# Output matmuls ahead of the scores of their pair, expert blocks written out, new orders in the prologue

## The chip, the cores and the metric

The kernel runs on one NeuronCore of one Trainium2 chip. The metric is the device time of one execution in microseconds (us); lower is better. Times of the engines come from one execution recorded by the hardware profiler.

## The reference

One layer: cross attention of 2048 latents on 1601 context rows and on the latents themselves, then a mixture of experts. All numbers are float32.

```python
# x: (1, 2048, 256), ctx: (1, 1601, 192), mask: (1, 1601)
xn = layernorm(ctx, ln_x_g, ln_x_b)
ln = layernorm(_layernorm(x), ln_l_g, ln_l_b)
q = ln @ Wq.T
kv = concatenate([xn @ Wkv.T, ln @ Wlkv.T], axis=1)      # 1601 + 2048 keys
qn = rmsnorm(q, qn_g) * 64 ** -0.5                        # 4 heads of 64
kn = rmsnorm(k, kn_g)
attn = softmax(where(full_mask, qn @ kn.T, -max))
x = x + (attn @ v) @ Wo.T + bo
h = _layernorm(x)
probs = softmax(h @ router_w.T)                           # 8 experts
weights, indices = top_k(probs, 2); weights = weights / (sum + 1e-6)
gate, up = split(h @ w13[e]);  y = (silu(gate) * up) @ w2[e]
x = x + sum over the two experts of weight * y
```

## The kernel before

Keys are padded to 29 tiles of 128 (13 of context, 16 of latents). The kernel has three stages, each written as one instruction stream per engine, with semaphores between the streams. Each engine runs its own stream strictly in order: an instruction that waits holds all behind it. Nothing is planned at run time; all orders are those of the code.

**Prologue** (0 to about 150 us). For each of the 29 tiles, in a pipeline: VectorE normalises rows (`apply`), TensorE transposes them into bX, ScalarE copies them to xT with scale and bias, TensorE projects them (bA: keys and queries, bV: values), ScalarE squares the keys (bSq), VectorE sums (`ss`), ScalarE takes the root (`nrm`), VectorE divides (knat, qn), TensorE transposes the keys (bK), ScalarE copies them to S2 (`s2`), and GpSimd copies their high part into S1 (`keys_hi`) while VectorE forms the low part (`klo`). Each engine has its own function `pro` (TensorE from L1327, ScalarE from L671, VectorE from L945), called with a step s; a part of a later stage works on tile s-2, s-3 or s-4. TensorE's projections wait for `xT` of the tile and for `knat` of the tile two before. Then GpSimd clears half of Q2 (L519, L521, semaphore `q20`), and TensorE computes the first unit's score maxima.

**Attention** (about 150 to 790 us). 16 units: 4 blocks of 512 queries times 4 heads. A unit has 15 steps p, each with a pair of key tiles (the last with one). In a step TensorE computes `scores(p)` into one of two double banks bS (two matmuls per tile, L1474 and L1475), ScalarE takes the exponential of the pair into PT (one of four buffers, L824), and GpSimd or VectorE adds PT to the running sums of the denominators (acc_p, acc_d). `outputs(p)` multiplies PT with V into bPV (L1485; a float32 matmul is seen as two records). TensorE does outputs in twos: at each odd p above 1 those of p-3 and p-2; the last three at the unit's end. Outputs of p wait for the exponential of p; scores of p wait for that of p-2.

Besides, unit v = u+1 needs the maximum of its scores beforehand. Therefore 32 `pieces` (L1401) of 464 keys for 128 queries are computed during unit u, into two banks bM in turn, and VectorE reduces each to a maximum (L1041, mpart). A piece waits until the reduction of the piece two before it is done:

```python
pe.wait_ge(sem("m_red"), NM * v + k + 1 - len(banks))
```

`PIECES` gives two counts for each step, `pieces(p, 0)` and `pieces(p, 1)`:

```python
PIECES = ((1, 0), (2, 0)) + ((1, 0), (2, 2)) * 5 + ((2, 0), (2, 0), (0, 0))
```

After the last piece VectorE forms the maximum (L1047), TensorE transposes it (`c_T`, L1407) and ScalarE copies it (`c_row`), on which the next unit's first scores wait. Other small work of the previous head or block is put at fixed steps: the transposed outputs and their division at 5 (`o_T` L1416, `o_out` L1053 and L1058), heads at 7, the output projection of one tile at 8, its second layer norm at 8 to 10, its transposes at 11, the router's logits at 12. On VectorE these come ahead of the reductions of their step. The last unit has no pieces; there VectorE also does all sums of the denominators and a part of the routing.

**Experts** (about 793 to 1045 us). The 4096 pairs of token and expert, sorted by expert, are 39 blocks of 128 rows. GpSimd gathers a block's rows (xg), TensorE transposes them (bXe, L1633), computes gate and up (bG, bU), transposes the product (bH, L1612) and computes bY (L1595 to L1597 are the three products of `three`); GpSimd adds the rows to the output by a scatter. TensorE reads the expert's number from `eid` into a register and addresses the weights W with it. `eid` packs three following numbers in base 8; blocks 5 to 38 are a hardware loop (`Fori`) of 17 passes with two blocks and one such read.

Of the kernel before, what the change touches and what calls it, by code (L numbers as in the profile page):

```python
# [4 lines left out]
F32 = mybir.dt.float32  # L5
# [4 lines left out]
ALU = mybir.AluOpType  # L10
ACT = mybir.ActivationFunctionType
AX = mybir.AxisListType.X

P = 128
# [115 lines left out]
def build(nc, x, ctx_in, mask, ln_x_g, ln_x_b, ln_l_g, ln_l_b, qn_g, kn_g, w_lat, w_ctx, wo_t, bo,  # L130
# [13 lines left out]
    with stack:  # L144
# [314 lines left out]
        def _(pool):  # L459
# [42 lines left out]
            for t in range(NK + 2):  # L502
                if t < NC + 2:
                    k_mask(t)
                    pool.wait_ge(sem("kmask"), t + 1)
                if t + 4 < NK:
                    rest_zero(t + 4, t + 5)
                    pool.wait_ge(sem("s20"), t + 2)
                if t == 3:
                    pool.wait_ge(sem("c_bo"), 16)  # L510
                    pool.wait_ge(sem("x_in"), 16)
                if 3 <= t < 3 + NT:
                    x_bias(t - 3)
                    pool.wait_ge(sem("xb"), t - 2)
                if t >= 2:
                    keys_hi(t - 2)
                    pool.wait_ge(sem("s1"), t - 1)
            pool.wait_ge(sem("v_mm"), NK)
            pool.memset(Q2[D:P, :, :].bitcast(F32), 0.0).then_inc(sem("q20"), 1)  # L519
            pool.wait_ge(sem("q20"), 1)  # L520
            pool.memset(Q2[D:D + 2, :, :].bitcast(F32), 1.0).then_inc(sem("q20"), 1)  # L521
            pool.wait_ge(sem("q20"), 2)
# [135 lines left out]
        def _(act):  # L658
            act.dma_start(wc[0:P, 0, :], w_ctx[0:P, :]).then_inc(sem("wc_in"), 16)
            act.dma_start(wc[0:CIN - P, 1, :], w_ctx[P:CIN, :]).then_inc(sem("wc_in2"), 16)  # L660
            for n, g in enumerate((ln_x_g, ln_x_b)):
                for k in range(2):
                    r = min(P, CIN - k * P)
                    act.dma_start(cols[0:r, 2 * n + k:2 * n + k + 1],
                                  g[k * P:k * P + r].rearrange("(p a) -> p a", a=1)).then_inc(sem("cols"), 16)

# [4 lines left out]
            def pro(s, a, b, c, q=0):  # L671
                if a:
                    act.wait_ge(sem("xT_mm"), s.v + 1)
                    if not (s.i is None and s.off < 2):
                        act.wait_ge(sem("v_mm"), s.v - 1)
                    for k in range(2):
                        r = P if (k == 0 or a == 'l') else CIN - P
                        g0 = 0 if a == 'c' else 4
                        act.activation(xT[0:r, s.par, k, :], bX[s.par][0:r, 0, k * P:(k + 1) * P], ACT.Identity,  # L679
                                       scale=cols[0:r, g0 + k:g0 + k + 1], bias=cols[0:r, g0 + 2 + k:g0 + 3 + k])\  # L680
                            .then_inc(sem("xT"), 1)
# [14 lines left out]
                if b:  # L696
                    act.wait_ge(sem("v_mm"), t.v + 1)
                    if b == 'l':
                        act.wait_ge(sem("xb"), t.back(NC).v + 1)
                    act.copy(V[:, bass.ds(t.v, 1), :].rearrange("p a d -> p (a d)"), bV[t.par][:, 0, 0:DIM])\  # L700
                        .then_inc(sem("v_cp"), 1)
                if q:
# [8 lines left out]
                if b:  # L711
                    lo = 0 if b == 'l' else H
                    act.wait_ge(sem("ss"), t.v + 1)
                    act.activation(nrm[:, lo:2 * H], ss[:, lo:2 * H], ACT.Sqrt, scale=1.0 / D)\
                        .then_inc(sem("nrm"), 1)
# [189 lines left out]
        def _(dve):  # L905
# [378 lines left out]
            link(dve.scalar_tensor_tensor(zt[:, 0:w], ef[:, 2:NBLK], float(E * E), zt[:, 0:w], ALU.mult, ALU.add))  # L1284
            dve.tensor_copy(eid[:], zt[:]).then_inc(sem("routed"), 1)
# [38 lines left out]
        def _(pe):  # L1324
# [134 lines left out]
            def unit(w):  # L1459
# [46 lines left out]
                for p in range(NP):  # L1506
                    scores(p)
# [16 lines left out]
                    if p % 2 and p > 1:  # L1524
                        outputs(p - 3)
                        outputs(p - 2)
# [73 lines left out]
            def experts(b):  # L1600
                v = pe.value_load(eid[0:1, bass.ds(b, 1)], min_val=0, max_val=E ** 3 - 1)
                return v % E, v // E % E, v // (E * E)
# [43 lines left out]
            e0, e1, _ = experts(0)  # L1646
            ffn(Step(None, 1), 1, 1, 0, e0, None)
            ffn(Step(None, 2), 1, 1, 1, e1, e0)
            e1, e2, e3 = experts(1)
            ffn(Step(None, 3), 1, 1, 1, e2, e1)  # L1650
            ffn(Step(None, 4), 1, 1, 1, e3, e2)
            with pe.Fori(0, (NBLK - 5) // 2) as i:
                eh, eg, en = experts(2 * i + 3)
                ffn(Step(i, 5), 1, 1, 1, eg, eh)
                ffn(Step(i, 6), 1, 1, 1, en, eg)
            eh, eg, _ = experts(NBLK - 2)
            ffn(Step(None, NBLK), 0, 1, 1, eg, eh)
            ffn(Step(None, NBLK + 1), 0, 0, 1, None, eg)

# [12 lines left out]
RING_FROM = 5  # L1672
POOL_SUMS = ((0, 1),) + tuple((-1, p) for p in (2, 3, 6, 7, 8, 10, 11, 12))
# [35 lines left out]
```

## Time and profile before

| | before |
|---|---|
| time, median of 3 runs (us) | 1047.28 (1045.42 to 1048.57) |
| profiled execution: its own time / its span (us) | 1047.05 / 1045.2 |
| TensorE matmuls busy | 965.9 us, 92% |
| TensorE weight loads busy | 626.4 us, 60% |
| VectorE busy | 695.8 us, 67% |
| ScalarE busy | 488.5 us, 47% |
| GpSimd busy | 593.6 us, 57% |
| mean granted TensorE clock, share of full speed | 0.978 |
| chain that ended last | PE 71%, DVE 10%, issue 6%, DMA 5%, ACT 4% |

PE is TensorE's matmuls, PEld its weight loads, DVE VectorE, ACT ScalarE, POOL GpSimd. The span is from the first to the last recorded instruction; the execution's own time has some 2 us around it. Matmuls overlap in the records, so a matmul's own duration is longer than the distance to the next. The chain is the work that ended last, followed back from the end; in it each matmul has the time that it adds.

### The profile page before, as it was taken

To read this page: it belongs to the slowest core of one execution; us is meant where nothing else is said; L and a number is where in the kernel's file an instruction comes from. 1 tells how busy PE (TensorE), PEld (TensorE's weight loads), DVE (VectorE), ACT (ScalarE), POOL (GpSimd) and SP (SyncE) were. 2 spreads that over 40 slices of the span, in tenths; PEclk is the share of its full clock that TensorE was granted. 3 is DMA by queue.
4 is the path that set the end of the run, shared out by engine and by line. 5 is a ranking of instruction groups with operands and counts; after the bars stand their busy time and mean duration, and the time that the engine had idled before them with its cause. 6 is when DMAs were issued, how large, how long until landed. Compare 5 with 4: busy or idle time off the path is not lost.

```text
span 1045.2 us, 15560 instructions
## 1 busy us (share of the span) xinstructions
PE 965.9 (92%) x4571; PEld 626.4 (60%) x4572; DVE 695.8 (67%) x1353; ACT 488.5 (47%) x782; POOL 593.6 (57%) x497
## 2 busy tenths in 40 slices
PE   5798779999999999999999999999997799999994
PEld 4555445556556555556556656565555687778883
DVE  5977677776776776776776776767786544444442
ACT  3565534554555465555555645655552232222231
POOL 2553227677677667666776676676800355555552
PEclk9999979999999999999999999999997999999998
DMA  6110021112122122222221221221248467663332
GB/s 188 40 37 6 18 87 66 57 61 68 54 66 76 61 76 72 65 66 64 74 71 61 66 81 56 72 75 62 94 179 302 129 161 165 153 136 54 53 52 25
DMA packets 72479, 87.51 MB, mean 84 GB/s; under 512 B 11399, under 2 KB 65608, under 8 KB 71400
## 3 DMA queue, kind: packets, MB, share of 16 engines
q1 hardware_dynamic: 56424, 70.73, 20.7%
q0 software_dynamic: 7488, 10.39, 6.2%
q10 hardware_dynamic: 8512, 5.71, 1.8%
q8 instruction: 28, 0.46, 0.2%
q14 instruction: 27, 0.22, 0.1%
HBM read 50.03 MB, written 36.77 MB: 83 GB/s over the span
## 4 chain that ended last, share of the span: by engine, by line
PE 71%; DVE 10%; issue 6%; DMA 5%; ACT 4%; POOL 2%; ACTq 1%; POOLq 0%; DVEq 0%
PE bPV L1485 20%; PE bM L1401 10%; PE bS L1474 9%; PE bS L1475 8%; DVE mpart L1041 2%; PE bA L1344 2%; DMA xg<-xln_d,ring_g 2%; ACT PT L824 2%; PE bT L1416 2%; PE bG L1595 1%; PE bY L1595 1%; PE bY L1597 1%; PE bY L1596 1%; PE bH L1612 1%; PE bV L1361 1%
## 5 line engine op out<-in xcount | busy, mean ns | idle before, releaser
L1041 DVE TENSOR_REDUCE mpart<-bM 128x1 f32<-128x464 f32 x490 | 294.5, 635 | 127.1 <-PE bM L1401 125.7
L535 POOL TENSOR_TENSOR acc_p<-acc_p,PT 128x1024 f32<-128x1024 f32 x120 | 302.9, 2524 | 103.8 <-ACT PT L824 100.4
L824 ACT ACTIVATE PT<-bS 128x1024 f32<-128x1024 f32 (+1 forms) x240 | 237.5, 997 | 199.8 <-PE bS L1475 170.6
L1485 PE MATMUL bPV<-PT,V 128*64 128x512 f32 x928 | 230.6, 604 | 0.0
L1474 PE MATMUL bS<-QQ,S 128*128 128x512 f32 x464 | 189.5, 408 | 3.6 <-ACT QQ L745 1.1
L1475 PE MATMUL bS<-QQ,S 128*128 128x512 f32 x464 | 183.7, 396 | 0.0
L1401 PE MATMUL bM<-S,QQ 128*128 128x464 f32 x490 | 172.2, 410 | 7.2 <-DVE mpart L1041 7.1
L1401 PEld LDWEIGHTS bM<-S,QQ 128*128 128x128 f32 x490 | 84.3, 191 | 90.3 <-DVE mpart L1041 69.8
L1485 PEld LDWEIGHTS bPV<-PT,V 128*64 128x64 f32 x928 | 58.7, 136 | 104.4 <-issue 92.3
L1474 PEld LDWEIGHTS bS<-QQ,S 128*128 128x128 f32 x464 | 87.7, 189 | 55.3 <-issue 26.7
L1475 PEld LDWEIGHTS bS<-QQ,S 128*128 128x128 f32 x464 | 87.8, 189 | 14.1
L539 POOL TENSOR_TENSOR wraw<-wraw,whi 128x256 fp32r<-128x256 f32 x96 | 85.2, 888 | 12.3 <-ACT whi L779 12.3
L1073 DVE TENSOR_TENSOR acc_d<-acc_d,PT 128x1024 f32<-128x1024 f32 (+1 forms) x58 | 88.3, 1523 | 1.3 <-ACT PT L824 0.6
L535 POOL TENSOR_TENSOR acc_p<-PT 128x1024 f32<-128x1024 f32 x15 | 38.4, 2559 | 86.9 <-ACT PT L824 86.9
L779 ACT CAST whi<-wraw 128x256 fp32r<-128x256 f32 x96 | 38.5, 402 | 84.5 <-DMA wraw<-w 83.9
L642 POOL DMA_INDIRECT out<-ysb,ring_s x34 | 54.4, 1601 | 34.5 <-POOL ring_s L635 23.0
L1298 DVE TENSOR_TENSOR hs<-hs,bU 128x512 f32<-128x512 f32 x39 | 26.8, 688 | 62.8 <-PE bU L1597 56.6
L886 ACT CAST hTe<-bH 128x512 fp32r<-128x512 f32 x39 | 22.9, 586 | 69.0 <-PE bH L1612 47.3
L618 POOL DMA_INDIRECT xg<-xln_d,ring_g x34 | 34.4, 1012 | 27.1 <-POOL ring_g L614 27.1
L1595 PE MATMUL bY<-W,hTe 128*128 x156 | 47.2, 303 | 1.5 <-DVE hTe L1292 1.5
L679 ACT ACTIVATE xT<-bX,cols 128x128 f32<-128x128 f32 (+1 forms) x58 | 23.2, 452 | 45.5 <-PE bX L1332 41.7
L1596 PE MATMUL bY<-W,hTe 128*128 x156 | 44.0, 282 | 0.0
(246 smaller groups left out, 1467.8 us busy)
## 6 DMA issues: line engine op xcount, KB each, us to landing
wraw<-w SPq DMA_DIRECT2D x96, 128.0 KB, 2.4
wsp_d<-whi SPq DMA_DIRECT2D x96, 128.0 KB, 2.4
wsp_d<-wraw SPq DMA_DIRECT2D x96, 128.0 KB, 1.7
W<-wsp_d SPq DMA_DIRECT2D x8, 1536.0 KB, 9.2
W<-wsp_d SPq DMA_DIRECT2D x32, 384.0 KB
V<-x SPq DMA_DIRECT2D x1, 2048.0 KB, 11.3
xb_d<-xbs SPq DMA_DIRECT2D x16, 128.0 KB, 1.7
x<-xb_d ACTq DMA_DIRECT2D x12, 128.0 KB, 2.0
```

The lines of the kernel that those rows point to most:

```text
L535: pool.tensor_tensor(acc_p[:], one, PT[:, q % NPT, :, :], ALU.add).then_inc(sem("z_p"), 1)
L539: pool.tensor_tensor(wraw[:, n % 2, :].bitcast(F32R), wraw[:, n % 2, :], whi[:, n % 2, :].bitcast(F32), ALU.subtract).then_inc(sem("wsplit ...
L642: pool.indirect_dma_start(out, bass.IndirectOffsetOnAxis(ap=rows, axis=0), ysb[:, s.par, :], None, compute_op=ALU.add)\
L824: act.activation(PT[:, p % NPT, 0:n, :], bS[(w.h + p) % 2][:, 0:n, :], ACT.Exp).then_inc(sem("exp"), 1)
L1041: dve.tensor_reduce(mpart[:, i, g:g + 1], banks[k % len(banks)][:, 0:PIECE], AX, ALU.max)\
L1073: dve.tensor_tensor(acc_d[:, 0:m, :], one, PT[:, q % NPT, 0:m, :], ALU.add).then_inc(sem("z_d"), 1)
L1401: pe.matmul(banks[k % len(banks)][:, 0:PIECE], Q2[:, h % 2, i * P:(i + 1) * P], S2[:, h, g * PIECE:(g + 1) * PIECE], start=True, stop=True ...
L1474: pe.matmul(bS[sl][:, b, :], S1[:, h, c * P:(c + 1) * P], Q1[:, h % 2, :], start=True, stop=False)
L1475: last = pe.matmul(bS[sl][:, b, :], S2[:, h, c * P:(c + 1) * P], Q2[:, h % 2, :], start=False, stop=True)
L1485: last = pe.matmul(bPV[b * D:(b + 1) * D, 0, :], V[:, c, h * D:(h + 1) * D], PT[:, p % NPT, b, :], start=c < 2, stop=c >= NK - 2, skip_gro ...
L1595: pe.matmul(out_ap, st_hi, w[:, s, 0, lo:lo + n], start=first, stop=False)
L1596: pe.matmul(out_ap, st_lo, w[:, s, 0, lo:lo + n], start=False, stop=False)
```

## The change

Five parts:

1. Attention, TensorE: in every unit `outputs(p-3)` and `outputs(p-2)` stand ahead of `scores(p)` instead of between `pieces(p, 0)` and `pieces(p, 1)`. `PIECES` and the banks stay.
2. Experts, TensorE: the loop is replaced by all blocks written out; a read of `eid` brings five expert numbers (8 reads). VectorE packs two more numbers into `eid`.
3. Prologue, ScalarE's `pro`: squares, key copy, norm, value copy, then the tile's copy xT, then queries. Before: xT first and the norm last.
4. Prologue, ScalarE's DMA issues: the four column loads ahead of the two of wc.
5. Prologue, GpSimd: the clears of Q2 at loop step 28, ahead of `keys_hi(26)`, instead of behind the loop.

```diff
@@ gpsimd
+                if t == NK - 1:
+                    pool.wait_ge(sem("v_mm"), NK)
+                    pool.memset(Q2[D:P, :, :].bitcast(F32), 0.0).then_inc(sem("q20"), 1)
+                    pool.wait_ge(sem("q20"), 1)
+                    pool.memset(Q2[D:D + 2, :, :].bitcast(F32), 1.0).then_inc(sem("q20"), 1)
+                    pool.wait_ge(sem("q20"), 2)
                 if t >= 2:
                     keys_hi(t - 2)
                     pool.wait_ge(sem("s1"), t - 1)
-            pool.wait_ge(sem("v_mm"), NK)
-            pool.memset(Q2[D:P, :, :].bitcast(F32), 0.0).then_inc(sem("q20"), 1)
...
@@ scalar
-            act.dma_start(wc[0:P, 0, :], w_ctx[0:P, :]).then_inc(sem("wc_in"), 16)
-            act.dma_start(wc[0:CIN - P, 1, :], w_ctx[P:CIN, :]).then_inc(sem("wc_in2"), 16)
             for n, g in enumerate((ln_x_g, ln_x_b)):
...
+            act.dma_start(wc[0:P, 0, :], w_ctx[0:P, :]).then_inc(sem("wc_in"), 16)
+            act.dma_start(wc[0:CIN - P, 1, :], w_ctx[P:CIN, :]).then_inc(sem("wc_in2"), 16)
...
             def pro(s, a, b, c, q=0):
-                if a:
-                    act.wait_ge(sem("xT_mm"), s.v + 1)
...
                 if b:
+                    lo = 0 if b == 'l' else H
+                    act.wait_ge(sem("ss"), t.v + 1)
+                    act.activation(nrm[:, lo:2 * H], ss[:, lo:2 * H], ACT.Sqrt, scale=1.0 / D)\
+                        .then_inc(sem("nrm"), 1)
+                if b:
                     act.wait_ge(sem("v_mm"), t.v + 1)
...
+                if a:
+                    act.wait_ge(sem("xT_mm"), s.v + 1)
...
@@ vector
+            for n in (3, 4):
+                w = NBLK - n
+                link(dve.scalar_tensor_tensor(zt[:, 0:w], ef[:, n:NBLK], float(E ** n), zt[:, 0:w], ALU.mult, ALU.add))
             dve.tensor_copy(eid[:], zt[:]).then_inc(sem("routed"), 1)
@@ tensor
                 for p in range(NP):
+                    if p % 2 and p > 1:
+                        outputs(p - 3)
+                        outputs(p - 2)
                     scores(p)
...
                     pieces(p, 0)
-                    if p % 2 and p > 1:
-                        outputs(p - 3)
-                        outputs(p - 2)
                     pieces(p, 1)
...
-            def experts(b):
-                v = pe.value_load(eid[0:1, bass.ds(b, 1)], min_val=0, max_val=E ** 3 - 1)
-                return v % E, v // E % E, v // (E * E)
+            order = []
+            def experts():
+                v = pe.value_load(eid[0:1, len(order):len(order) + 1], min_val=0, max_val=E ** AHEAD - 1)
+                for n in range(AHEAD):
+                    order.append((v // E ** n if n else v) % E)
...
-            with pe.Fori(0, (NBLK - 5) // 2) as i:
-                eh, eg, en = experts(2 * i + 3)
-                ffn(Step(i, 5), 1, 1, 1, eg, eh)
-                ffn(Step(i, 6), 1, 1, 1, en, eg)
...
+            for b in range(1, NBLK + 2):
+                if len(order) < min(b + 1, NBLK):
+                    experts()
+                ffn(Step(None, b), b < NBLK, b <= NBLK, b > 1, order[b - 1], order[b - 2])
+AHEAD = 5
```

## Rows read from the trace of the kernel before

**Rows 1.** Waits of TensorE, 155 to 790 us: total us, times, longest.

```profile
PE bM L1401 <- DVE mpart L1041: 6.9, 12, 1.9
```

**Rows 2.** Busy us by window: length, PE, PEld, DVE, ACT, POOL, granted clock, DMA.

```profile
0.00:50.00 50.00, 33.40 (x153) 24.23 (x155) 36.99 (x133) 23.29 (x68) 20.73 (x49) 1.00 0.38 117
...
100.00:110.00 10.00, 9.20 (x38) 5.33 (x37) 6.56 (x17) 6.51 (x18) 1.72 (x3) 1.00 0.00 0
...
140.00:150.00 10.00, 6.17 (x15) 3.31 (x15) 6.88 (x16) 3.08 (x5) 1.45 (x2) 0.50 0.30 95
```

**Rows 3.** Chain of waits, steps 5 to 7 of a unit: start us, us added.

```profile
357.06 0.53 PE bM L1401 x2
357.58 1.87 PE bPV L1485 x8
359.45 0.62 PE bM L1401 x2
...
362.13 0.42 PE bM L1401 x2
```

**Rows 4.** Timeline, step 13 and step 5: start us, us, instruction, idle before and releaser.

```profile
338.80 0.78 PE L1401 MATMUL bM<-S,QQ 128*128 128x464 f32 x2
...
339.21 1.19 DVE L1041 TENSOR_REDUCE mpart<-bM 128x1 f32<-128x464 f32 x2
340.44 0.19 DVE L1047 TENSOR_REDUCE cells<-mpart 128x4 f32<-128x32 f32 x1
340.54 3.69 DVE L1073 TENSOR_TENSOR acc_d<-acc_d,PT 128x1024 f32<-128x1024 f32 x2
...
357.31 0.42 DVE L1058 TENSOR_TENSOR on<-bT,cells 128x256 f32<-128x256 f32 x1
```

**Rows 5.** Timeline around a piece of step 9 that waits.

```profile
367.95 1.82 DVE L1041 TENSOR_REDUCE mpart<-bM 128x1 f32<-128x464 f32 x3
...
368.61 0.19 PEld L1401 LDWEIGHTS bM<-S,QQ 128*128 128x128 f32 x1 [0.86 <-DVE mpart L1041]
368.61 0.47 PE L1401 MATMUL bM<-S,QQ 128*128 128x464 f32 x1 [0.45 <-DVE mpart L1041]
...
369.02 1.94 PE L1485 MATMUL bPV<-PT,V 128*64 128x512 f32 x8
```

**Rows 6.** Timeline of TensorE, step 2 to step 3.

```profile
348.71 0.38 PE L1401 MATMUL bM<-S,QQ 128*128 128x464 f32 x1
349.22 0.50 PE L1474 MATMUL bS<-QQ,S 128*128 128x512 f32 x1
```

**Rows 7.** Timeline of VectorE, last unit, first sum.

```profile
763.75 1.23 DVE L1073 TENSOR_TENSOR acc_d<-PT 128x1024 f32<-128x1024 f32 x1 [3.38 <-PE bT L1417]
```

**Rows 8.** Timeline of TensorE, prologue: projections of latent tiles.

```profile
56.32 1.95 PE L1344 MATMUL bA<-wl,xT 128*128 128x512 f32 x4
...
104.74 1.95 PE L1344 MATMUL bA<-wl,xT 128*128 128x512 f32 x4 [0.71 <-ACT xT L679]
108.27 1.95 PE L1344 MATMUL bA<-wl,xT 128*128 128x512 f32 x4
```

**Rows 9.** Timeline, end of the prologue: first piece and first reduction.

```profile
127.94 1.91 PE L1401 MATMUL bS<-S,QQ 128*128 128x464 f32 x4 [3.20 <-POOL QQ L521]
...
128.73 2.28 DVE L1041 TENSOR_REDUCE mpart<-bS 128x1 f32<-128x464 f32 x4 [2.16 <-PE bS L1401]
```

**Rows 10.** Waits of TensorE, experts, 830 to 1030 us: total us, times, longest.

```profile
PE bH L1612 <- issue: 4.8, 10, 0.6
```

**Rows 11.** Timeline of TensorE, experts: transposes of single blocks.

```profile
941.29 0.60 PE L1612 MATMUL bH<-ident,hs 128*128 128x128 f32 x4
...
1002.67 0.60 PE L1612 MATMUL bH<-ident,hs 128*128 128x128 f32 x4
1007.54 0.60 PE L1612 MATMUL bH<-ident,hs 128*128 128x128 f32 x4
...
1023.30 0.63 PE L1612 MATMUL bH<-ident,hs 128*128 128x128 f32 x4
```

More of the change, by code:

```diff
@@ L517, in _ @@
                     pool.wait_ge(sem("s1"), t - 1)
-            pool.wait_ge(sem("v_mm"), NK)
-            pool.memset(Q2[D:P, :, :].bitcast(F32), 0.0).then_inc(sem("q20"), 1)
-            pool.wait_ge(sem("q20"), 1)
-            pool.memset(Q2[D:D + 2, :, :].bitcast(F32), 1.0).then_inc(sem("q20"), 1)
-            pool.wait_ge(sem("q20"), 2)
             NZ = len(POOL_SUMS)
@@ L671, in pro @@
             def pro(s, a, b, c, q=0):
-                if a:
-                    act.wait_ge(sem("xT_mm"), s.v + 1)
[L674 to L681, printed above, removed]
                 if b:
@@ L701, in pro @@
                         .then_inc(sem("v_cp"), 1)
+                if a:
+                    act.wait_ge(sem("xT_mm"), s.v + 1)
+                    if not (s.i is None and s.off < 2):
+                        act.wait_ge(sem("v_mm"), s.v - 1)
+                    for k in range(2):
+                        r = P if (k == 0 or a == 'l') else CIN - P
+                        g0 = 0 if a == 'c' else 4
+                        act.activation(xT[0:r, s.par, k, :], bX[s.par][0:r, 0, k * P:(k + 1) * P], ACT.Identity,
+                                       scale=cols[0:r, g0 + k:g0 + k + 1], bias=cols[0:r, g0 + 2 + k:g0 + 3 + k])\
+                            .then_inc(sem("xT"), 1)
                 if q:
@@ L710, in pro @@
                                    ACT.Identity, scale=gT[:, 0:1]).then_inc(sem("qT"), 1)
[L711 to L715, printed above, removed]
             lo, hi = CTX_LOADS[0]
@@ L1645, in _ @@
             pe.wait_ge(sem("routed"), 1)
[L1646 to L1651, printed above, removed]
-            with pe.Fori(0, (NBLK - 5) // 2) as i:
-                eh, eg, en = experts(2 * i + 3)
-                ffn(Step(i, 5), 1, 1, 1, eg, eh)
-                ffn(Step(i, 6), 1, 1, 1, en, eg)
-            eh, eg, _ = experts(NBLK - 2)
-            ffn(Step(None, NBLK), 0, 1, 1, eg, eh)
-            ffn(Step(None, NBLK + 1), 0, 0, 1, None, eg)
+            for b in range(1, NBLK + 2):
+                if len(order) < min(b + 1, NBLK):
+                    experts()
+                ffn(Step(None, b), b < NBLK, b <= NBLK, b > 1, order[b - 1], order[b - 2])
 CTX_LOADS = ((0, 4), (4, NC - 1))
```

## Prediction

> **What bounds the kernel now.** I read the page first: TensorE is busy 966 us of 1045 (the table above), and what it waits for in the attention stage (155 to 790 us) is almost nothing; the table of waits puts 6.9 us down to the reductions of the piece maxima, its largest item [rows 1]. So there an instruction that TensorE runs costs its length, a new wait costs in full, and a mere change of order is worth only the waits it removes. The stage is 16 units of 38 to 41 us, seen as the starts of their last output matmuls. Then I read the chain of waits through one pair of steps. Output matmuls of two steps take 1.87, two pieces after them 0.62, and two pieces before them 0.42: a piece is 0.21, and 0.20 is paid once on leaving the outputs. The pair of steps repeats after 357.58 to (362.13 + 0.42) = 4.97, without a gap [rows 3].
>
> **Attention: where four pieces now meet.** A step's pieces are two counts, (2, 2) at steps 3, 5, 7, 9 and 11; the outputs stood between the two. Now outputs come before the scores, and the four pieces follow each other. There are two bM banks, and piece k waits until the reduction of k-2 is done. Before, 1.87 us of outputs covered two reductions. Worked out from the first piece's start at 0, with nothing between them:
> - the reduction of a starts 0.41 later (338.80 to 339.21), and one takes 0.61 (1.82 for three) [rows 4, 5]: a is free at 1.02, b at 1.63;
> - c starts at 1.06 and d at 1.68: 0.05 after a reduction ends (the first of the three from 367.95 ends at 368.56, the waiting piece starts at 368.61);
> - a piece that waited takes 0.41 until the next matmul (368.61 to 369.02), not 0.21, as its weight load starts with it [rows 5]. The next scores start at 2.09.
>
> Four pieces unhindered take 0.84, so a group loses 1.25. The 0.20 on leaving the outputs is then paid by the scores: no change. Bounds: 1.0 if both loads were hidden, 1.35 if a reduction's start slips a little. At step 5 VectorE first runs the division of the finished head: it ends at 357.73, 0.67 after the piece that the chain has at 357.06 [rows 3, 4], so a's reduction starts about 0.3 later and that group loses 1.55 (in 14 of the 15 units that have pieces). A pieces' unit loses 4 x 1.25 + 1.55 = 6.55.
>
> The weight load has a rule. The row shows the load of the waiting piece at 368.61, not earlier [rows 5]. The Trainium skill, TensorE: Matmul & The Clock Gate, "Architectural detail: the array is 16x 32x32, not 1x 128x128", says that TensorE's queue can pull weight loads ahead of matmuls in flight. By it both loads would hide and the total would be 75 x 2 x 0.2 = 30 us lower, an estimate; the row speaks against it, as the wait holds the load too.
>
> **Attention: the end of a unit.** Step 13 had pieces, outputs 10 and 11 (1.87), scores 14, then the transposes of the maxima. Its two pieces now end the piece work directly ahead of scores 14 (0.46, two matmuls). VectorE ends the second reduction at 0.41 + 1.22 = 1.63 and its maximum of 0.19 follows [rows 4] at about 1.85; TensorE is there at 0.42 + 0.46 = 0.88. That is 1.0 of wait. From there outputs 12 to 14 (2.7) lead to the next unit, while VectorE still has two sums (3.69 [rows 4]) and two merges (some 1.9 more, by the same rate). Its first reduction comes some 0.6 late and holds the second piece of step 1: another 0.5. So 1.55 per unit, from 0.6 to 2.2.
>
> **Attention: what the order gives back.** Scores 3 wait for exp 1 at the start of a unit: the piece at 348.71 would be done at 348.92, scores start at 349.22 with a slower first one [rows 6]; the outputs of step 0 now fill this: 0.4 in 15 units. The piece at step 9 that waits at 368.61 (VectorE is behind with the statistics of step 8) has outputs ahead of it now: the wait of 0.45 and the load of 0.2 go, 0.7 in 11 units. Step 13's pieces cost 0.2 more than free ones, 15 times. Unit 0 has one wait of 1.9 of the same kind. Together 6 + 7.7 + 3 + 1.9 = 18.6.
>
> Sum for units 0 to 14: 15 x 6.55 - 0.3 + 15 x 1.55 - 18.6 = +102.6. In the last unit, which has no pieces, VectorE's first sum waits for the transposed output of step 5 and starts at 763.75 after 3.38 idle [rows 7]. Two outputs (1.87) now stand before that, and the exponentials wait for the sums. But step 11's wait for the normalised tile then covers the same 1.87. I take +0.7, from -1.5 to +2.5. Attention: +103.
>
> **Prologue.** For latent tiles TensorE starts a tile every (104.74 - 56.32) / 12 = 4.03 us; where it waits for nothing the distance is 108.27 - 104.74 = 3.53 [rows 8]. The loop is: ScalarE waits for the transpose of tile s before it squares tile s-2, the norm comes last in its step, and TensorE waits for the normalised key. In the new order squares, key copy and norm come first, and the tile copy behind them needs only what is there; ScalarE and VectorE, busy 6.5 and 6.6 us in 10 [rows 2], so 2.6 per tile of 4.03, stay below 3.53 with their gaps closed. Behind the tile copy wait TensorE's projections, one step later, with 1 us to spare. 15 tiles x 0.45 = 6.5, from 2 to 7.5. Context tiles: the timeline has VectorE, which also does the statistics of x there, without a gap from 24 to 47 us, so nothing there; an estimate of 1.5 in the last three and 1 at the start, by the gaps VectorE has in them. The DMA order: the columns' loads go ahead of wc and land perhaps 1 us sooner, wc (384 KB) is queued later behind x and may land 1 to 1.5 after the columns. Net 0, between -1.5 and +1.5. The Q2 clears: the first pieces wait for them at 127.94 after 3.20 idle, the first reduction is at 128.73 [rows 9]. They now run as soon as the last V matmul is done (about 119.5), while GpSimd waits for keys; the three key copies behind them can slip by the clears' 1.9 and catch up, as each waits for ScalarE. What then sets the first reduction is VectorE's own key and query work, free 2.16 before it [rows 9]: gain 2.1, up to 3.1, nothing if these copies are late. Prologue: -11, from -4 to -14.
>
> **Experts.** Loop passes show as idle before the first transposes of odd blocks: 4.8 us in 10 gaps, "issue", up to 0.6 [rows 10], and the load exposed beside them. Undisturbed blocks are 1007.54 - 1002.67 = 4.87 apart; 16 blocks from 941.29 to 1023.30 take 5.13 each, 4.1 in all over the floor [rows 11]. The first 18 blocks lose about as much again to it and also wait for gathers, which GpSimd and the weight DMAs set; there a removed gap mostly turns into a longer gather wait. Eight loads of the expert numbers stay, at a gap of about 0.4 each. So 3 from the second half, 1 from the first: -4, from +3 (straight code served worse than the loop) to -8. Two more VectorE instructions of 0.2 before "routed" lie beside the first gather. The end is a chain of scatters that follows TensorE: it moves with it.
>
> The gap itself: by the row 0.2 to 0.6 at a pass. The Trainium skill, Advanced Engine Details and Errata, "Control Flow Timing", gives about 51 ns for a branch and 108 ns for a compare and branch; 17 passes would be an estimated 2.7 us, and the written out code would bring 1 us instead of 4. The rows say that more than the branch is lost.
>
> **Sum.** +103 - 11 - 4 = +88 on the profiled execution: span 1045.2, its own time 1047.05, which is 0.2 below the median of the three runs. 1047 + 88 = 1135.
>
> **Rivals.**
> - *The pieces don't hold the queue* (faster). If scores could start past a waiting piece, four pieces in a row would be free, and the returned waits (18.6), prologue and experts would remain: 1047 - 19 - 11 - 4 = 1013. It decides from the point at which VectorE is at most 0.5 behind TensorE at a group's end. For it: VectorE is only 67% busy. Against: at 368.61 the outputs, which need nothing of that piece, waited behind it [rows 5]. 4%.
> - *One wait in a group, not two*: if reduction a started with its bank's own end, c would hardly wait; 0.6 per group instead of 1.25: 75 x 0.65 = 49 less, 1086. Row 339.21 is against it. 7%.
> - *The clock.* If the new gaps lowered the granted clock, TensorE would run at 1.2 GHz of 2.4 in part. It was 0.50 in 140 to 150, a window in which TensorE was busy 6.2 us and waited long for the last reductions, and 1.00 over the first 50 us with 33 us busy [rows 2]. My gaps are up to 1.2. A tenth of the stage at half speed adds about 60: 1195. 4%.
> - *The unit's end recovers nothing and reductions slip*: everything at its upper bound in attention, 75 x 0.1 + 15 x 0.65 = +17, and half the prologue's gain: 1158. 10%.
>
> My forecast has 75%. For the range: the likeliest with its bounds runs from 1112 to 1152; I widen it a little to 1106 and 1156, which leaves out the rivals at 1013, 1086 and 1195 and part of the last. A difference below 0.3% (3 us) can't be told from none. Faster 0.05, same 0.01, slower 0.94.
>
> **What would show it.** The waits table of after: "PE bM from DVE mpart" at 70 to 100 us instead of 7, in some 150 places, with two of about 0.6 in a group; the pair of steps at 6.2 instead of 4.97; a unit at 45 to 48; latent tiles 3.5 to 3.6 apart; the first reduction of unit 0 about 10 us earlier; no idle time before transposes of experts except at one block in five. The forecast is wrong if the four pieces stand in the timeline without gaps, if the pair of steps stays near 5, or if the granted clock in attention is below 1.

## The result, and the profile after

| | before | after |
|---|---|---|
| median of the runs, us | 1046.57 | 1135.74 (1135.29 to 1136.63) |
| ratio after / before | | 1.085, interval 1.083 to 1.087 |
| span of the profiled execution, us | 1045.2 | 1133.5 |
| mean granted TensorE clock | 0.978 | 0.961 |

The changed kernel is 8.5% slower; 1135 was predicted. The stages of the two traces, each from one mark to the next (the "end" of a unit is the start of its ten last output matmuls):

| stretch | before | after | difference | predicted |
|---|---|---|---|---|
| start to the first reduction of a piece | 128.7 | 113.4 | -15.3 | -11 |
| to the end of unit 0, then of unit 14 | 57.5 + 564.3 | 62.0 + 660.7 | +4.5 + 96.4 | +102.6 |
| to the first output of the tail (last unit) | 42.5 | 46.1 | +3.6 | +0.7 |
| tail and router to the first gather | 26.1 | 26.1 | 0 | 0 |
| experts | 226.0 | 225.2 | -0.8 | -4 |

The sum is right to 1 us, but three of its terms (prologue, last unit, experts) were not, as the last two columns show, and inside attention's term errors met that the section on the prediction takes apart. First the waits of TensorE in attention after (total us, times, longest), against [rows 1]:

```profile
PE bM L1405 <- DVE mpart L1042: 41.3, 73, 0.8
PE bT L1411 <- DVE cells L1048: 13.6, 15, 0.9
PE bS L1478 <- ACT PT L825: 3.6, 3, 2.5
```

The wait of a piece for the reduction of the piece two before it went from 6.9 to 41.3 us, and a wait of the transposes of the maxima (bT), 0.9 in each of 15 units, is new. The rest of the loss is not in this table, because it is in weight loads. The timeline of a group of four shows it (start us, us, instruction, idle before and releaser); it is to be read beside [rows 3, 5] of the kernel before:

```profile
367.40 0.58 PE L1405 MATMUL bM<-S,QQ 128*128 128x464 f32 x2
...
367.81 2.40 DVE L1042 TENSOR_REDUCE mpart<-bM 128x1 f32<-128x464 f32 x4 [2.23 <-PE bM L1405]
368.50 0.19 PEld L1405 LDWEIGHTS bM<-S,QQ 128*128 128x128 f32 x1 [0.91 <-DVE mpart L1042]
368.50 1.02 PE L1405 MATMUL bM<-S,QQ 128*128 128x464 f32 x2 [0.52 <-DVE mpart L1042]
...
369.05 0.19 PEld L1405 LDWEIGHTS bM<-S,QQ 128*128 128x128 f32 x1 [0.36 <-DVE mpart L1042]
...
369.36 0.39 PE L1478 MATMUL bS<-QQ,S 128*128 128x512 f32 x1
```

Two pieces run, the third stands until the first reduction is over (0.52), the fourth issues its load late too (PEld row 369.05). From the first piece to the scores it is 369.36 - 367.40 = 1.96 us; four free pieces take 0.84. The load of a piece that waits starts with it, at 368.50 as in [rows 5]: the pull-ahead of the Trainium skill (TensorE: Matmul & The Clock Gate, "Architectural detail: the array is 16x 32x32, not 1x 128x128") does not reach past a wait of this kind here either.

At step 5 VectorE's division of the finished head comes first, and in this unit the clock then falls:

```profile
375.20 0.67 PE L1405 MATMUL bM<-S,QQ 128*128 128x464 f32 x2
375.59 0.42 DVE L1059 TENSOR_TENSOR on<-bT,cells 128x256 f32<-128x256 f32 x1
...
376.61 1.30 PE L1405 MATMUL bM<-S,QQ 128*128 128x464 f32 x2 [0.75 <-DVE mpart L1042]
377.71 0.63 PE L1478 MATMUL bS<-QQ,S 128*128 128x512 f32 x1
378.14 0.63 PE L1479 MATMUL bS<-QQ,S 128*128 128x512 f32 x1
```

The group takes 2.51, 1.67 more than a free one. From 377.71 the scores are 0.43 apart, before they were 0.23 (a matmul's record 0.63 against 0.39). The windows (length, PE, PEld, DVE, ACT, POOL, granted clock, DMA) say why, the granted clock being 0.86 in the first and 1.00 in the next. Taken by single us it is 0.50 from 377 to 380:

```profile
370.00:382.00 12.00, 11.21 (x49) 6.12 (x48) 5.60 (x10) 3.38 (x4) 4.62 (x4) 0.86 0.21 67
382.00:394.00 12.00, 10.82 (x44) 6.14 (x44) 7.02 (x15) 6.09 (x8) 8.17 (x5) 1.00 0.18 60
```

The wait of 0.75 alone does not decide it. In unit 1 of the same trace the group of step 5 starts at 192.56 and has the same wait, but the granted clock stays 1.00 (190 to 197 us), the group takes 2.28 and the scores behind it are 0.23 apart:

```profile
192.56 0.67 PE L1405 MATMUL bM<-S,QQ 128*128 128x464 f32 x2
193.98 1.02 PE L1405 MATMUL bM<-S,QQ 128*128 128x464 f32 x2 [0.75 <-DVE mpart L1042]
194.84 0.40 PE L1478 MATMUL bS<-QQ,S 128*128 128x512 f32 x1
```

Units 2 and 4 are like unit 1; in the other 11 of the 14 units with this wait the clock falls. What else it takes stays open.

The unit's end, beside [rows 4] (DVE L1048 is the maximum over the pieces, L1074 the sums, L1411 the transposes that wait for the maximum):

```profile
404.80 1.94 DVE L1074 TENSOR_TENSOR acc_d<-acc_d,PT 128x1024 f32<-128x1024 f32 x2
405.03 0.60 PE L1411 MATMUL bT<-ident,cells 128*1 128x128 f32 x4 [0.91 <-DVE cells L1048]
```

The two sums take 1.94 here and took 3.69 before, because there the first began while GpSimd was running two of its own (337.16 to 342.00), as this row of the kernel before shows; *e5_three* below says what that does:

```profile
337.16 4.84 POOL L535 TENSOR_TENSOR acc_p<-acc_p,PT 128x1024 f32<-128x1024 f32 x2
```

Prologue and last unit, against [rows 8, 9] and [rows 7]: the first and the last latent tile, the first reduction, the first sum of the last unit.

```profile
52.16 1.88 PE L1348 MATMUL bA<-wl,xT 128*128 128x512 f32 x4
...
103.15 1.88 PE L1348 MATMUL bA<-wl,xT 128*128 128x512 f32 x4
...
113.41 1.17 DVE L1042 TENSOR_REDUCE mpart<-bS 128x1 f32<-128x464 f32 x2
...
851.27 1.23 DVE L1074 TENSOR_TENSOR acc_d<-PT 128x1024 f32<-128x1024 f32 x1 [6.35 <-PE bT L1421]
```

### The profile page after: what moved, and what is told of

It reads as the page before. It is cut to its first block, busy times and chain, and to the rows that moved or that the text cites. A ratio compares the mean times of both kernels' runs of the same rounds, so it can differ in the third digit from the quotient of the medians.

```text
span 1133.5 us, 15379 instructions
## 1 busy us (share of the span) xinstructions
PE 1007.7 (89%) x4571; PEld 628.6 (55%) x4571; DVE 673.1 (59%) x1355; ACT 484.7 (43%) x782; POOL 578.4 (51%) x497
## 4 chain that ended last, share of the span: by engine, by line
PE 65%; DVE 16%; DMA 8%; issue 6%; POOL 2%; ACT 1%; POOLq 1%; ACTq 0%; DVEq 0%
PE bPV L1489 20%; PE bS L1478 12%; DVE mpart L1042 10%; PE bS L1479 9%; PE bM L1405 8%; DMA xg<-xln_d,ring_g 4%; PE bA L1348 3%; DMA out<-ysb,ring_s 2%; PE bV L1365 2%; PE bT L1420 1%; POOL ring_g L615 1%; DMA out<-ysb,sidx 1%; PE bT L1421 1%; PE bT L1432 1%; PE bT L1411 1%
## 5 line engine op out<-in xcount | busy, mean ns | idle before, releaser
L1405 PE MATMUL bM<-S,QQ 128*128 128x464 f32 x490 | 192.6, 435 | 47.3 <-DVE mpart L1042 42.3
L1489 PE MATMUL bPV<-PT,V 128*64 128x512 f32 x928 | 234.6, 613 | 0.0
L1478 PE MATMUL bS<-QQ,S 128*128 128x512 f32 x464 | 201.1, 434 | 4.7 <-ACT PT L825 3.6
L1479 PE MATMUL bS<-QQ,S 128*128 128x512 f32 x464 | 189.0, 407 | 0.0
L1405 PEld LDWEIGHTS bM<-S,QQ 128*128 128x128 f32 x490 | 92.6, 196 | 112.3 <-DVE mpart L1042 100.3
L1478 PEld LDWEIGHTS bS<-QQ,S 128*128 128x128 f32 x464 | 90.8, 196 | 108.8 <-issue 80.1
L1479 PEld LDWEIGHTS bS<-QQ,S 128*128 128x128 f32 x464 | 90.8, 196 | 14.0
L540 POOL TENSOR_TENSOR wraw<-wraw,whi 128x256 fp32r<-128x256 f32 x96 | 70.8, 738 | 14.4 <-ACT whi L780 14.4
L1074 DVE TENSOR_TENSOR acc_d<-acc_d,PT 128x1024 f32<-128x1024 f32 (+1 forms) x58 | 62.2, 1072 | 1.4 <-ACT PT L825 0.6
L1599 PE MATMUL bY<-W,hTe 128*128 x156 | 47.5, 305 | 1.5 <-DVE hTe L1296 1.5
L619 POOL DMA_INDIRECT xg<-xln_d,ring_g x34 | 34.4, 1013 | 27.1 <-POOL ring_g L615 25.5
L1601 PE MATMUL bY<-W,hTe 128*128 x156 | 44.0, 282 | 0.0
L1600 PE MATMUL bY<-W,hTe 128*128 x156 | 44.0, 282 | 0.0
```

Of the source, the lines that this page charges most:

```text
L540: pool.tensor_tensor(wraw[:, n % 2, :].bitcast(F32R), wraw[:, n % 2, :], whi[:, n % 2, :].bitcast(F32), ALU.subtract).then_inc(sem("wsplit ...
L1074: dve.tensor_tensor(acc_d[:, 0:m, :], one, PT[:, q % NPT, 0:m, :], ALU.add).then_inc(sem("z_d"), 1)
L1405: pe.matmul(banks[k % len(banks)][:, 0:PIECE], Q2[:, h % 2, i * P:(i + 1) * P], S2[:, h, g * PIECE:(g + 1) * PIECE], start=True, stop=True ...
L1478: pe.matmul(bS[sl][:, b, :], S1[:, h, c * P:(c + 1) * P], Q1[:, h % 2, :], start=True, stop=False)
L1479: last = pe.matmul(bS[sl][:, b, :], S2[:, h, c * P:(c + 1) * P], Q2[:, h % 2, :], start=False, stop=True)
L1489: last = pe.matmul(bPV[b * D:(b + 1) * D, 0, :], V[:, c, h * D:(h + 1) * D], PT[:, p % NPT, b, :], start=c < 2, stop=c >= NK - 2, skip_gro ...
```

## Experiments

Ratios are to the kernel before in the same session (medians 1046.9, 1045.95 and 1046.0).

### Each part alone

*e1_order*: the kernel before with only this edit (the same in the change).

```diff
                 for p in range(NP):
+                    if p % 2 and p > 1:
+                        outputs(p - 3)
+                        outputs(p - 2)
                     scores(p)
...
                     pieces(p, 0)
-                    if p % 2 and p > 1:
-                        outputs(p - 3)
-                        outputs(p - 2)
                     pieces(p, 1)
```

> The kernel before with the new order of the attention units alone. Theory: all of the loss is in it: two waits of the four pieces in a group on their reductions (75 groups of 1.1 to 1.7 us), one wait of the transposed maxima in each unit (0.9), a lower granted clock for some 3 us in most units (1.4 each), 3.6 in the last unit: before + 100 to 106 us, about 1151, with TensorE waiting 40 to 45 us for mpart. Rival: part of the loss comes from code that grew by the written out experts, or from a prologue that ends earlier; then this kernel loses under 95 us.

Measured: 1150.2 us, ratio 1.099 (1.096 to 1.101), clock 0.963. The order alone costs 103.

*e2_prologue*: ScalarE's new order in a prologue step, the column loads first and the early Q2 clears, without the rest.

> The kernel before with the three prologue changes alone. Theory: the 15.3 us by which the first reduction came earlier (128.73 to 113.41) are kept to the end: 1031 to 1033. Rival: they are given back, as the weight conversion of the first chunks or a lower clock holds the first unit: 1036 or more.

Measured: 1030.8, ratio 0.984 (0.983 to 0.986). It gains 16.1, and attention behind it does not take it back.

*e3_experts*: the expert blocks written out for TensorE, with the expert numbers five to a load.

> The kernel before with the written out expert blocks alone. Theory: GpSimd's gathers and scatters set the pace there, so that removed loop gaps come back as gather waits: 1044.5 to 1047, and TensorE waits about 10 us for gathers instead of 2.7. Rival: the gaps' 5 to 9 us are won and the changed kernel lost them only to its later start: 1038 to 1042.

Measured: 1046.95, ratio 1.0002 (0.999 to 1.002). Together 103 - 16 + 0 = 87, against 89 measured for the whole: the parts add.

*e10_act*: of the prologue only ScalarE's order: squares, key copy, norm and V copy ahead of the tile copy.

```diff
             def pro(s, a, b, c, q=0):
-                if a:
-                    act.wait_ge(sem("xT_mm"), s.v + 1)
...
                 if b:
+                    lo = 0 if b == 'l' else H
+                    act.wait_ge(sem("ss"), t.v + 1)
...
+                if a:
+                    act.wait_ge(sem("xT_mm"), s.v + 1)
```

> The kernel before with ScalarE's new order in the prologue alone (squares, key copy, norm, V copy, then the tile copy); column loads and the Q2 clears as before. Theory (the loop through ScalarE set the distance of the tiles): latent tiles 3.5 apart instead of 4.03 and the last context tiles closer: 8 to 11 us of the prologue's 16: 1036 to 1039. Rival (the gain came mainly from the columns' earlier loads and the clears): 1041 or more.

Measured: 1032.3, ratio 0.987 (0.985 to 0.989), a gain of 13.7, more than the theory's 8 to 11; the rival's 1041 or more is out. Its tiles are as close as in the whole change:

```profile
96.86 1.88 PE L1344 MATMUL bA<-wl,xT 128*128 128x512 f32 x4
100.32 1.88 PE L1344 MATMUL bA<-wl,xT 128*128 128x512 f32 x4
```

3.46 apart. What remains for the clears and the columns is some 2 us.

### What in the new order costs

*e6_half*: the changed kernel; every reduction but those of unit 0 reads half a piece.

```diff
-banks[k % len(banks)][:, 0:PIECE], AX, ALU.max)
+banks[k % len(banks)][:, 0:PIECE // 2 if v else PIECE], AX, ALU.max)
```

> The changed kernel, but the reductions of the piece maxima read 232 of the 464 columns in all pieces but those of unit 0: half of every piece is left out of the maxima; TensorE's work is unchanged. Theory (each group loses what two reductions last beyond the pieces): a reduction takes about 0.35 instead of 0.61, the third piece can start 0.77 after the first instead of 1.1 and the fourth does not wait: the group of four loses about 0.55 instead of 1.12, 75 groups, 40 us less, and the clock's 15 us largely return: 1078 to 1100 us. Rival (the loss is in the weight loads that a stopped queue exposes, or in VectorE's place, not in the length of the reduction): the time stays above 1120.

Measured: 1082.7, ratio 1.036 (1.034 to 1.039): 53 us less than the changed kernel. TensorE's waits in attention and a reduction:

```profile
PE bM L1405 <- DVE mpart L1042: 23.5, 72, 0.5
```
```profile
L1042 DVE TENSOR_REDUCE mpart<-bM 128x1 f32<-128x232 f32 x330 | 119.1, 394 | 163.8 <-PE bM L1405 163.5
```

The same matmuls stand in the same order, and the waits shrink with the reduction (mean 394 ns against 635 ns); part of the 53, some 14, is the clock, 0.974 over the run, which falls at step 5 in one unit instead of 11. A group of four takes 1.49 instead of 1.97. So the length of VectorE's reduction sets the price of the order. The price is not gone: the group still loses 0.65, and the run stays 37 above the kernel before, although its prologue gained 16.

*e9_fill*: the changed kernel with two matmuls in the gap of step 5.

```diff
                     pieces(p, 0)
+                    if p == OUT_AT and not w.first and not w.last:
+                        pe.wait_ge(sem("exp"), NP * u + p)
+                        for _ in range(2):
+                            pe.matmul(bS[(h + p + 1) % 2][:, 0, :], S2[:, h, 0:P], Q2[:, h % 2, :], start=True, stop=True)
                     pieces(p, 1)
```

> The changed kernel with two matmuls into a free bank of the scores between the second and the third piece of step 5, in units 1 to 14: there TensorE stood idle for 0.75 us, and from there the granted clock was 0.5 for some us. The added matmuls' result is not used. Theory (the clock falls after this gap): granted clock in attention back to 0.99 to 1.00, up to 15 us less than the changed kernel: 1120 to 1126 us. Rival 1 (the clock falls for another reason, the whole pattern of gaps): it falls at another place as often, 1133 to 1139. Rival 2 (the added matmuls push the pieces and VectorE's reductions back): above 1139.

Measured: 1121.0, ratio 1.071 (1.070 to 1.073), clock 0.978 (0.961 in the changed kernel): 15 us less for 28 matmuls more. The same window as above, and the group of step 5:

```profile
370.00:382.00 12.00, 11.12 (x54) 6.46 (x50) 5.97 (x11) 4.11 (x6) 5.65 (x4) 1.00 0.21 67
```
```profile
374.29 0.67 PE L1405 MATMUL bM<-S,QQ 128*128 128x464 f32 x2
374.79 0.62 PE L1534 MATMUL bS<-QQ,S 128*128 128x512 f32 x2
375.70 1.03 PE L1405 MATMUL bM<-S,QQ 128*128 128x464 f32 x2 [0.29 <-DVE mpart L1042]
376.58 0.40 PE L1478 MATMUL bS<-QQ,S 128*128 128x512 f32 x1
```

The idle time before the third piece is 0.29 instead of 0.75, and in units 1 to 14 the granted clock no longer falls to 0.5. The third piece starts as late after the first as in the changed kernel (375.70 - 374.29 = 1.41 = 376.61 - 375.20): the wait for VectorE is the same, only filled. The group takes 2.29, so that 0.22 of the 2.51 above were the clock. So some 15 of the 105 us in attention were the clock, and the gap of step 5 was what it hung on.

*e5_three*: the changed kernel, pieces dealt out (2, then 3 in a row) per pair of steps instead of (1, then 4).

```diff
-PIECES = ((1, 0), (2, 0)) + ((1, 0), (2, 2)) * 5 + ((2, 0), (2, 0), (0, 0))
+PIECES = ((1, 0), (2, 0)) + ((2, 0), (2, 1)) * 5 + ((2, 0), (2, 0), (0, 0))
```

> The changed kernel with its pieces dealt out anew: two in every even step and three, instead of four, in a row behind the scores of an odd step (five per pair of steps as before). Theory (two bM banks, the reduction of k-2 must be over): in the trace of the changed kernel the first piece of a group starts at 367.40, the third at 368.50 after a wait of 0.52, the fourth at 369.05, the next scores at 369.36. With three the scores follow the third piece at about 369.0: 0.3 less per group, 75 groups, 22 us, and part of the 15 us by the lower granted clock comes back: 1100 to 1117 us, wait on the reductions of the maxima 25 to 40 us instead of 42 at PE. Rival (what costs is that four or three outputs, scores and pieces of two steps stand together, so that VectorE's list is late whatever the number of pieces): 1130 or more.

Measured: 1120.4, ratio 1.070 (1.068 to 1.072). 15 less, just outside the theory's 1117. The group of three behaves as the theory says where nothing else disturbs it: it takes 1.42 and loses 0.79, for 1.12 with four. But 12 of the 75 take 2.31 to 2.33, the wait is larger than thought (52.6 us, up to 1.4), and the granted clock is not given back (0.963). The timelines of VectorE and GpSimd at step 7 show the cause, first of this kernel, then of the changed one:

```profile
379.62 2.38 POOL L536 TENSOR_TENSOR acc_p<-acc_p,PT 128x1024 f32<-128x1024 f32 x1 [5.87 <-ACT PT L825]
379.77 3.31 DVE L1074 TENSOR_TENSOR acc_d<-PT 128x1024 f32<-128x1024 f32 x1
...
383.00 1.84 DVE L1042 TENSOR_REDUCE mpart<-bM 128x1 f32<-128x464 f32 x3
...
383.68 0.47 PE L1405 MATMUL bM<-S,QQ 128*128 128x464 f32 x1 [1.42 <-DVE mpart L1042]
```
```profile
380.60 1.22 DVE L1074 TENSOR_TENSOR acc_d<-PT 128x1024 f32<-128x1024 f32 x1
380.82 3.23 POOL L536 TENSOR_TENSOR acc_p<-acc_p,PT 128x1024 f32<-128x1024 f32 x1 [7.38 <-ACT PT L825]
```

Whichever sum starts first keeps its length (2.38 on GpSimd, 1.22 on VectorE) and the other lasts until the first is done and its own length more: 379.62 + 2.38 + 1.22 = 383.22, against 383.08 read. All 19 of VectorE's sums in this trace that began beside a running one of GpSimd's end within 0.2 of that rule, and so do the 15 of the kernel before. Here GpSimd was first, and the reductions behind VectorE's sum came 2 us late. The Trainium skill has this rule (SBUF — State Buffer, "SBUF: two separate sides"): a VectorE operation with two SBUF inputs and a GpSimd operation share a port pair as an exclusive lock, and the later one blocks. The traces agree.

### Another order, and VectorE's list

*e4_alt*: the changed kernel, two pieces directly behind the outputs, then the scores, then one piece.

```diff
                         outputs(p - 3)
                         outputs(p - 2)
+                        pieces(p, 0)
                     scores(p)
...
-                    pieces(p, 0)
+                    if not (p % 2 and p > 1):
+                        pieces(p, 0)
                     pieces(p, 1)
...
-PIECES = ((1, 0), (2, 0)) + ((1, 0), (2, 2)) * 5 + ((2, 0), (2, 0), (0, 0))
+PIECES = ((1, 0), (2, 0)) + ((2, 0), (2, 1)) * 5 + ((2, 0), (2, 0), (0, 0))
```

> The changed kernel, but an odd step does outputs, pieces, scores, pieces (two and one), an even step scores and two pieces: outputs still stand ahead of the scores, and never more than two pieces follow each other. Theory: the run of four pieces is the cost, not the outputs ahead of scores: no wait on reductions inside groups, granted clock 1.0 in attention, pair of steps 4.97: 1022 to 1034. Rival: outputs ahead of scores cost by themselves (later exponentials, later sums, later step 5 output): 1060 or more.

Measured: 1100.1, ratio 1.050 (1.047 to 1.053), clock 0.963. The theory failed: groups of two are not free, and the time is the rival's (1060 or more). Steps 5 and 7 of a unit:

```profile
411.97 0.42 DVE L1059 TENSOR_TENSOR on<-bT,cells 128x256 f32<-128x256 f32 x1
...
413.00 0.47 PE L1405 MATMUL bM<-S,QQ 128*128 128x464 f32 x1 [1.28 <-DVE mpart L1042]
...
415.74 3.32 DVE L1074 TENSOR_TENSOR acc_d<-PT 128x1024 f32<-128x1024 f32 x1
...
419.67 0.48 PE L1405 MATMUL bM<-S,QQ 128*128 128x464 f32 x1 [1.01 <-DVE mpart L1042]
```

VectorE's list has other work ahead of the reductions in a step (the division, the sum, at step 11 the norm), and TensorE waits for it. That the 1.87 us of outputs between the groups absorbed this in the old order is read from the orders and was not tried by itself.

*e11_first*: e4_alt with the reductions first in each step of VectorE.

```diff
                 for p in range(NP):
+                    if not w.last:
+                        for _ in range(sum(PIECES[p])):
+                            piece(v, k, M_BANKS)
+                            k += 1
...
                     if p == OUT_AT and not w.first:
                         o_out(u, (w.h - 1) % H, w.pairs)
...
```

> The order of the alternative with two pieces straight behind the outputs (1100.1 us), and VectorE's list changed: in each step the reductions of the piece maxima come first, the division of the finished head, the sums, the statistics and the norm after them. Theory (what stands ahead of the reductions in VectorE's list caused the alternative's 45 us of waits: the division at step 5 with 1.28, the sum of 3.32 at step 7 with 1.01, the norm at step 11 with 0.88): the waits of TensorE on these reductions fall from 45 to under 12 us, the granted clock in attention to 0.99 or above, 1025 to 1050 us. Rival (the pieces behind the outputs are too dense for two banks and 0.61 a reduction, whatever else VectorE does): 1080 or more. Second rival (later sums and statistics hold ScalarE's buffers or the transposed outputs instead): waits on the reductions small, and 1055 to 1080.

Measured: 1062.7, ratio 1.015 (1.012 to 1.018), 37 less. The waits of TensorE and ScalarE in attention:

```profile
PE bM L1405 <- DVE mpart L1042: 16.5, 16, 1.5
```
```profile
ACT PT L825 <- DVE acc_d L1074: 34.4, 16, 7.5
```

The first line was 45.0 us, 40 times, in e4_alt; the theory had under 12, so it holds in the main but not in full. The second is new: the exponentials now wait for the later sums to free their tile. The time is the second rival's (1055 to 1080), not the theory's (1050 at most).

*e12_best*: the changed kernel with attention's old order and GpSimd's blocks written out (below). *e13_best_first*: that, with VectorE's reductions first.

> The changed kernel with attention's order put back to that of before, and GpSimd's gathers and scatters written out. Theory (the parts add up: prologue 16, experts with GpSimd written out 5): 1022 to 1028 us. Rival (the two gains share something, such as the DMA queues at the start of the experts): 1029 to 1033.

> The same kernel as e12_best with VectorE's reductions first in each step. Theory (the wait of 0.45 and the exposed load of 0.2 at step 9, 11 times, come from the statistics of step 8 ahead of the reductions): 5 to 8 us less than e12_best, PE's waits on these reductions under 3 us. Rival (the statistics move behind and hold the norm, the router or the sums; the order buys nothing): within 3 us of e12_best, or slower.

Measured: e12_best 1025.4, ratio 0.979 (0.977 to 0.981), the fastest of all. e13_best_first 1089.6, ratio 1.041 (1.039 to 1.043): 64 slower. The theory missed; the rival had "or slower" and the sums held, but nothing of this size. TensorE waits 40.0 us for these reductions instead of 6.1, and the clock is 0.960 against 0.975, so that a part is the clock. Its timeline (VectorE's sum at step 11, ScalarE's next exponential, the next piece):

```profile
302.95 5.69 POOL L536 TENSOR_TENSOR acc_p<-acc_p,PT 128x1024 f32<-128x1024 f32 x2
...
303.71 2.72 DVE L1075 TENSOR_TENSOR acc_d<-acc_d,PT 128x1024 f32<-128x1024 f32 x1
...
306.54 1.02 ACT L826 ACTIVATE PT<-bS 128x1024 f32<-128x1024 f32 x1 [1.77 <-DVE acc_d L1075]
307.03 0.63 PE L1406 MATMUL bM<-S,QQ 128*128 128x464 f32 x1 [1.78 <-DVE mpart L1043]
```

Put behind the reductions, the sum meets one of GpSimd's and lasts 2.72. The exponential that needs its tile waits (108 us in all, 32 times, in ScalarE's waits), and so do the reductions of the next step. This is read from the trace and was not tested by itself. The same edit that took 37 us from one order cost the other 64.

### The experts

Waits for the gathered rows in e3_experts, 830 to 1045 us, with the same line of the kernel before and of e8_pool behind it:

```profile
PE bXe L1640 <- DMA xg<-xln_d,ring_g: 9.9, 12, 2.7
```
```profile
PE bXe L1633 <- DMA xg<-xln_d,ring_g: 2.7, 5, 0.9
```
```profile
PE bXe L1641 <- DMA xg<-xln_d,gidx: 5.2, 8, 1.6
```

Where TensorE no longer loses 4.8 us to loop passes [rows 10], it waits 7.2 us more for gathers. In e3_experts GpSimd, which issues them, is never far ahead:

```profile
935.10 1.60 POOL L642 DMA_INDIRECT out<-ysb,ring_s  x1 [1.23 <-DMA out<-ysb,ring_s]
936.13 0.77 POOL L614 COPY ring_g<-gidx 128x1 int32 x1
937.70 1.01 POOL L618 DMA_INDIRECT xg<-xln_d,ring_g  x1 [0.79 <-POOL ring_g L614]
939.13 0.18 POOL L635 COPY ring_s<-sidx 128x1 int32 x1 [0.42 <-DVE ysb L1320]
940.23 1.60 POOL L642 DMA_INDIRECT out<-ysb,ring_s  x1 [0.92 <-POOL ring_s L635]
```

A block of GpSimd takes 940.23 - 935.10 = 5.1 us, of which the index copies that its loop needs, with the waits behind them, are 0.77 + 0.79 + 0.18 + 0.92 = 2.7. TensorE's undisturbed block is 4.87 [rows 11].

*e8_pool*: e3_experts with that loop written out, so that the copies go.

```diff
-                run_steps(pool, lo, hi, lambda s, a=a: step(s, *a))
+                for b in range(lo, hi):
+                    step(Step(None, b), *a)
```

> The kernel before with the expert blocks written out for TensorE (as in the experts alone, 1046.95 us) and GpSimd's loop of gathers and scatters written out too, so that its index copies (ring_g 0.77 + 0.8, ring_s 0.18 + 0.93 of a block's 4.82 us) are gone. Theory (GpSimd's loop paces the blocks, which is why the written out TensorE code alone gave nothing): gather waits of TensorE (9.9 + 17.0 us in the experts alone, 2.7 + 6.2 before) fall under 3, blocks at TensorE's own 4.85 or below, 1035 to 1041 us. Rival (weights' or the gathers' own transfers set the pace): 1045 to 1049.

Measured: 1040.9, ratio 0.995 (0.993 to 0.997). 5 us gained where TensorE's part alone gave none: GpSimd's loop held the blocks. Loop and copies went together, and GpSimd's part without TensorE's was not run, so whether TensorE's written out blocks add anything to the 5 us is open. The gather wait fell from 9.9 to 5.2 us, not under the theory's 3: GpSimd now stands 1.8 to 3.3 us before a scatter until the last one has landed.

## Why the prediction was right, and where not

**Groups of four: right.** Measured 1.12 for 1.25. At step 5 it is 2.29 - 0.84 = 1.45 for 1.55 (e9_fill; the 1.67 of the changed kernel has 0.22 of the clock in it). That is 4 x 1.12 + 1.45 = 5.93 per unit for 6.55. Two waits are there in each group, the first 0.52 long, the second only in the load (369.05); the sign of 70 to 100 us in TensorE's waits therefore came as 41.3. The last piece took 0.31 until the scores, where I had 0.41. e6_half shows that the reduction's length sets the loss.

**The unit's end: half right.** The transposes wait 0.91 where 1.0 was forecast. The second wait, 0.5 at step 1, never came: it rested on two sums of 3.69 [rows 4], and they now take 1.94. The 3.69 held time in which GpSimd's sums blocked them, not their own length alone. So gross 15 x (5.93 + 0.91) = 103 instead of 121.

**The clock: wrong, 15 us.** It was a rival of 4% and all or nothing (1195). It came in part: units 1 to 13 take 612.6 from end to end in the changed kernel and 598.6 in e9_fill, with the granted clock at 1.00. The step that failed is "My gaps are up to 1.2", weighed against a row with a much longer wait only [rows 2]: the granted clock fell after a wait of 0.75. The prediction had named a granted clock below 1 in attention as a sign that it is wrong; it was 0.97 from 140 to 837 us.

**Attention's sum: right by luck.** The waits' 103 and the clock's 15 give 118, and +100.9 was measured, so by difference the order gave back some 17, for the 18.6 forecast; this was not measured by itself. The waits were put 18 too high, the clock at nothing instead of 15, and what comes back 2 too high: +102.6 was near because these errors met.

**Last unit: too small.** +3.6 for +0.7, 1 above the upper bound. The first sum starts 1.95 later, counted from the last unit end, which is the 1.87 of outputs ahead of it. That step 11 would give this back did not happen. The other 1.7 is, as read from the trace, the clock again: behind a wait of TensorE of 2.45 for an exponential, the granted clock is 0.50 from 855 to 858 us, and in the chain eight matmuls of outputs add 3.52 instead of 1.87:

```profile
854.90 3.52 PE bPV L1489 x8
```

**Prologue: too small.** -15.3 for -11, a little beyond the bound. Latent tiles went from 60.16 / 15 = 4.01 apart to (103.15 - 52.16) / 15 = 3.40: 9.2 for 6.5 (the forecast's 15 x 0.45 is 6.75). The floor I took, 3.53, was the distance behind a tile that had waited 0.71 [rows 8]; it is not a floor, as the 3.46 and less of after show. The context tiles gave 4.2 (56.32 - 52.16) for 2.5. From the last tile to the first reduction it is 2.0 less for 2.1, as forecast. e10_act confirms the mechanism: ScalarE's order holds 13.7 of 16.

**Experts: -0.8 for -4.** That is inside the bounds, but the step "3 from the second half" failed. The loop gap was taken as lost time at TensorE, while the gathers of GpSimd stood right behind it. e3_experts and e8_pool show it.

**Rivals.** Pieces do hold the queue, and the first reduction starts 0.41 after the first piece, as in [rows 4] (367.40 and 367.81). Nothing of the 1013 and 1086 cases is seen.

## To carry to other kernels

With two banks between TensorE and VectorE, what counts is how many matmuls of that kind stand in a row, what else stands between the groups, and what the reader has ahead of them in its own list; spread them by the reader's time, 0.61 here, not by the writer's 0.21. Before a wait is removed on one engine, read who would be waited for next: writing out the expert loop of TensorE alone brought nothing (1046.95), with GpSimd's written out as well it was 5 us. A duration from a trace is the operation's own only where nothing beside it could block it; take it from the shortest of its kind.

## What the runs showed of the hardware

- After a wait of 0.75 us the scores ran 0.43 apart instead of 0.23 for some 2 us, the granted clock's lower level (1.2 GHz of 2.4), in 11 of 14 units, 1.4 us each. In the other three the same wait left the clock at 1.00. Two matmuls into that wait undid it (granted clock 0.86 to 1.00 from 370 to 382 us, time 1135.7 to 1121.0).
- VectorE's sum of 128x1024 takes 1.22 us alone and 3.31 when GpSimd's sum began 0.15 before it; GpSimd's takes 2.38 alone and 3.23 when VectorE's was first. Dealing out the pieces otherwise over the steps decided which.
